# Early fp16 tanh from partial sums and earlier injections in the last 73 Runge-Kutta steps of a conv, mixture and ODE block

## The reference, cut to what matters

```
def _mlp(y, W1, b1, W2, b2, W3, b3):
    h = jnp.tanh(y @ W1.T + b1)
    h = jnp.tanh(h @ W2.T + b2)
    return h @ W3.T + b3
def _rk4_step(y, dt, params):
    k1 = f(y)
    k2 = f(y + dt / 2 * k1)
    k3 = f(y + dt / 2 * k2)
    k4 = f(y + dt * k3)
    return y + dt * (k1 + 2 * k2 + 2 * k3 + k4) / 6
t = t + ode(layernorm(t))      # 16 images x 128 channels, hidden 512, 255 steps one after the other
```

## Time and profile before

| | us |
|---|---|
| median of 3 runs | 2869.14 (2864.23 to 2873.52) |
| profiled execution | 2866.97 |
| its span | 2864.70 |
| PE busy | 2798.6 (98%) |
| DVE busy | 2348.9 (82%) |
| ACT busy | 1553.5 (54%) |
| POOL busy | 774.5 (27%) |
| stretch of the plain steps with their entry, from 2121.4 to 2853.4 | 732.0 |

### The profile page before, as it was taken

How to read it: one execution, slowest core, us unless ns; L and a number is a source line. 1 busy time by engine, 2 the same in 40 slices (tenths; PEclk the granted TensorE clock), 3 DMA queues, 4 the chain that set the end, 5 groups by cost and what they waited for, 6 DMA issues and landing times.

```text
span 2864.7 us, 207841 instructions
## 1 busy us (share of the span) xinstructions
PE 2798.6 (98%) x81958; PEld 2399.7 (84%) x81958; DVE 2348.9 (82%) x13248; ACT 1553.5 (54%) x10132; POOL 774.5 (27%) x1393
## 2 busy tenths in 40 slices
PE   8799999999999999999999999999999999999999
PEld 4578888888888888888888887888889999999998
DVE  5688888888888888888888887888878888888887
ACT  7555555555555555555554444444445555555555
POOL 5833233233233233323322000111122222222222
PEclk9789999999999999999999999999999999999999
DMA  3000000000000000000000000000000000000000
GB/s 119 3 14 11 11 15 11 11 15 11 11 14 12 11 11 15 11 11 15 11 11 9 0 0 1 0 0 0 0 17 0 0 0 0 0 0 0 0 0 15
DMA packets 21984, 28.24 MB, mean 10 GB/s; under 512 B 4384, under 2 KB 12896, under 8 KB 21544
## 3 DMA queue, kind: packets, MB, share of 16 engines
q1 hardware_dynamic: 21928, 27.48, 3.1%
HBM read 25.24 MB, written 2.23 MB: 10 GB/s over the span
## 4 chain that ended last, share of the span: by engine, by line
PE 93%; DVE 3%; ACT 2%; issue 1%; DMA 0%; SPq 0%; POOLq 0%; DVEq 0%; POOL 0%; ACTq 0%
PE PSUM L702 23%; PE PSUM L708 21%; PE PSUM L910 17%; PE PSUM L763 12%; PE PSUM L693 5%; PE PSUM L906 4%; DVE PSUM L1427 1%; PE PSUM L800 1%; PE PSUM L866 1%; PE PSUM L871 1%; PE PSUM L729 1%; ACT HA L1100 1%; PE PSUM L733 1%; PE PSUM L770 1%; PE PSUM L523 0%
## 5 line engine op out<-in xcount | busy, mean ns | idle before, releaser
L1427 DVE TENSOR_REDUCE PSUM<-PSUM 128x32 f32<-128x64 f32 x2912 | 624.8, 232 | 97.4 <-PE PSUM L708 51.9
L702 PEld LDWEIGHTS PSUM<-HA,RL 128*128 128x128 f16 x11648 | 396.2, 96 | 205.8 <-ACT HA L1100 194.7
L1101 ACT ACTIVATE PSUM<-PSUM 128x32 f32<-128x32 f32 x2912 | 561.2, 194 | 0.0
L1100 ACT ACTIVATE HA<-PSUM 128x32 f16<-128x32 f32 x1456 | 289.0, 199 | 472.1 <-DVE PSUM L1427 472.0
L1100 ACT ACTIVATE HB<-PSUM 128x32 f16<-128x32 f32 x1456 | 289.2, 200 | 465.6 <-DVE PSUM L1427 465.5
L702 PE MATMUL PSUM<-HA,RL 128*128 128x16 f16 x11648 | 511.9, 170 | 15.5 <-ACT HA L1100 7.6
L702 PE MATMUL PSUM<-HB,RLU 128*128 128x16 f16 x11648 | 511.4, 170 | 3.7
L435 POOL TENSOR_TENSOR G<-G 128x512 f16<-128x512 f32 x256 | 296.9, 1160 | 683.1 <-ACT G L1073 683.1
L708 PE MATMUL PSUM<-HA,RH 128*128 128x32 f16 x11648 | 465.7, 177 | 0.0
L708 PE MATMUL PSUM<-HB,RHU 128*128 128x32 f16 x11648 | 464.4, 177 | 0.0
L702 PEld LDWEIGHTS PSUM<-HB,RLU 128*128 128x128 f16 x11648 | 393.8, 96 | 46.9 <-ACT HB L1100 2.0
(11 more groups left out here) (315 smaller groups left out, 6726.8 us busy)
## 6 DMA issues: line engine op xcount, KB each, us to landing
G<-scores SPq DMA_DIRECT2D x64, 256.0 KB, 3.1
N<-in_x SPq DMA_DIRECT2D x8, 256.0 KB, 4.7
NHL<-in_w SPq DMA_DIRECT2D x1, 2048.0 KB, 9.9
STF<-in_w SPq DMA_DIRECT2D x1, 2048.0 KB, 14.5
out<-W2HL SPq DMA_DIRECT2D x8, 256.0 KB, 2.4
G<-in_r SPq DMA_DIRECT2D x1, 1024.0 KB, 5.1
R1K<-in_r SPq DMA_DIRECT2D x1, 256.0 KB, 2.7
R3F<-in_r SPq DMA_DIRECT2D x1, 256.0 KB, 5.3
```

The costliest lines, as they stand in the source:

```text
L702: mm(out[m // 2][:, 2 * B * (m % 2):2 * B * (m % 2) + B], lo[:, k, m], src[:, k, 0], start=False, stop=False)
L1100: A(hi[:, 2 * h:2 * h + 2, 0], src, ACT.Tanh, scale=1.0 / scale).then_inc(rk_hi, 1)
L1101: A(full, src, ACT.Tanh, scale=1.0 / scale).then_inc(rk_f, 1)
L1427: v.tensor_reduce(bank[:, SUM:SUM + 2 * B].rearrange("p (m b) -> p m b", m=2), bank[:, 0:4 * B].rearrange("p (m c b) -> p m b c", m=2, c=2 ...
```

## The change

PE has a new order of the 40 products, in which the eight `l` stand last (places 32 to 39), and the other products of m = 0 and 1 end at place 19 (`h30`). The semaphore `sp_p[g]` now counts the end of a group without its `l`; a new one, `sp_all`, the end of the `l`. Ahead of the first `l`, PE waits until ACT has made the fp16 tanh of m0 and m1 of the next layer (`sp_hi[0]`, count + 1), since the `l` add to the sums that this tanh reads. The next layer's injection moves from between the layers to place 32, ahead of the `l`, or to place 36, after four of them, where j = 3 and in lay 0 of j = 0: three of the eight layers. The injection for the first layer of the next step is at the end of the loop's body, and one for the first plain step ahead of the loop.

ACT makes the fp16 tanh of m0 and m1 from sums without their `l`, that of m2 from the high half of its pair alone (without the low half, and without DVE's addition), and that of m3 from the full sum, as before. The full tanh follow, in the order m3, m0 and m1, m2. The low half, which is the difference of the two, takes up what the early tanh left out. DVE adds m3's pair first and m2's after ACT's early tanh of m2, subtracts in the order m3, m0 and m1, m2, and in lay 1 of j = 2 makes `FS` ahead of both additions to y instead of between them.

```diff
 SPLIT_ORDER = [(w[0], int(w[1]), int(w[2])) for w in (
-    "L11 L10 h00 L13 L00 h10 h11 h01 L01 L02 L12 h20 L21 L20 l10 l00 H12 l01 L32 h31 L30 h21 l11 l21 L31 H22 l20 "
...
+    "L03 L02 L11 L22 h10 L21 L20 h11 L23 L10 L30 h31 h20 h00 h21 h01 L00 L01 L31 h30 "
+    "L12 H33 L32 L33 L13 H13 H12 H03 H02 H23 H22 H32 l30 l00 l20 l21 l11 l01 l10 l31").split()]
+OPEN_NEXT_AT = (32, 36)
...
-            def split_layer(s, j, lay, hi, lo, src, opening):
-                waited = set()
+            def split_layer(s, j, lay, hi, lo, src, opening, open_next):
+                waited, after_read = set(), False
                 for i, (kind, k, m) in enumerate(SPLIT_ORDER):
+                    if i == OPEN_NEXT_AT[j == 3 or (j == 0 and lay == 0)]:
+                        open_next()
...
+                    if kind == "l" and not after_read:
+                        after_read = True
+                        pe.wait_ge(sp_hi[0], split_count(s, j, lay) + 1)
+                    rest = [(a, b) for a, _, b in SPLIT_ORDER[i + 1:] if SPLIT_OF[b] == SPLIT_OF[m]]
+                    ends = all((a == "l") != (kind == "l") for a, _ in rest)
...
-                        t.then_inc(sp_p[SPLIT_OF[m]], 1)
+                        t.then_inc(sp_all if kind == "l" else sp_p[SPLIT_OF[m]], 1)
+
+            def open_second(s, j):
+                pe.wait_ge(rk_s, 4 * s + j)
+                split_inject(1, IDV, CI[:, 3], True)
+
+            def open_first(s, j):
+                if j == 1:
+                    pe.wait_ge(rk_hs, s)
+                    state_high()
+                if j == 2:
+                    state_low()
+                pe.wait_ge(rk_u, 4 * s + j + 1)
+                if j in (0, 3):
+                    open_high(UZ if j == 0 else BZ, UI if j == 0 else BI)
+                else:
+                    if j == 2:
+                        pe.wait_ge(x_bl, s - S_PLAIN + 1)
+                    split_inject(0, IDU, UI if j == 1 else IB, True)
 
             def split_step(s, opening):
                 for j in range(4):
-                    pe.wait_ge(rk_s, 4 * s + j)
-                    split_inject(1, IDV, CI[:, 3], True)
-                    split_layer(s, j, 0, RH2, RL2, HA, opening and j == 0)
...
-                    split_layer(s, j, 1, RHU[:, COEF_OF[j]], RLU[:, COEF_OF[j]], HB, False)
-
+                    split_layer(s, j, 0, RH2, RL2, HA, opening and j == 0, lambda: open_first(s, j))
+                    split_layer(s, j, 1, RHU[:, COEF_OF[j]], RLU[:, COEF_OF[j]], HB, False,
+                                lambda: open_second(s, j + 1))
+
+            open_second(S_PLAIN, 0)
             split_step(S_PLAIN, True)
...
-                        for g, ms in enumerate(SPLIT):
-                            act.wait_ge((sp_r if g else sp_p)[g], split_count(s, j, lay))
-                            sl = slice(ms[0], ms[-1] + 1)
-                            A(hi[:, sl, 0], SPLIT_SUM[lay][:, sl], ACT.Tanh, scale=1.0 / scale).then_inc(sp_hi[g], 1)
+                        act.wait_ge(sp_p[0], split_count(s, j, lay))
+                        A(hi[:, 0:2, 0], SPLIT_SUM[lay][:, 0:2], ACT.Tanh, scale=1.0 / scale).then_inc(sp_hi[0], 1)
+                        act.wait_ge(sp_p[1], split_count(s, j, lay))
+                        A(hi[:, 2, 0], PAIRED[lay][0][:, 0:B], ACT.Tanh, scale=1.0 / scale).then_inc(sp_hi[1], 1)
+                        act.wait_ge(sp_r[2], split_count(s, j, lay))
+                        A(hi[:, 3, 0], SPLIT_SUM[lay][:, 3], ACT.Tanh, scale=1.0 / scale).then_inc(sp_hi[2], 1)
+                        for g, done in ((2, sp_r[2]), (0, sp_all), (1, sp_r[1])):
+                            act.wait_ge(done, split_count(s, j, lay))
+                            sl = slice(SPLIT[g][0], SPLIT[g][-1] + 1)
                             A(SPLIT_FULL[lay][:, sl], SPLIT_SUM[lay][:, sl], ACT.Tanh, scale=1.0 / scale).then_inc(sp_f[g], 1)
...
-                            for g in (1, 2):
+                            for g, ready in ((2, sp_p[2]), (1, sp_hi[1])):
                                 ms = SPLIT[g]
-                                dve.wait_ge(sp_p[g], split_count(s, j, lay))
+                                dve.wait_ge(ready, split_count(s, j, lay))
...
-                            for g, ms in enumerate(SPLIT):
+                            for g in (2, 0, 1):
...
-                            if j == 2:
-                                state(s)
...
                             if j == 2:
+                                state(s)
                                 state_end(s)
```

More of the change, by code:

```diff
@@ L90 @@
 SPLIT_ORDER = [(w[0], int(w[1]), int(w[2])) for w in (
-    "L11 L10 h00 L13 L00 h10 h11 h01 L01 L02 L12 h20 L21 L20 l10 l00 H12 l01 L32 h31 L30 h21 l11 l21 L31 H22 l20 "
-    "h30 H02 l30 l31 H32 L22 L03 H23 H33 H03 H13 L23 L33").split()]
+    "L03 L02 L11 L22 h10 L21 L20 h11 L23 L10 L30 h31 h20 h00 h21 h01 L00 L01 L31 h30 "
+    "L12 H33 L32 L33 L13 H13 H12 H03 H02 H23 H22 H32 l30 l00 l20 l21 l11 l01 l10 l31").split()]
+OPEN_NEXT_AT = (32, 36)
 def build(nc, scores, x, wkq, wv, wr, bkq, bv, br, wg, w1, b1, w2, b2, ck, cb, r1, r2, r3, r3n, rb1, rb2, rb3, ident,
@@ L260, in build @@
         sp_p, sp_r, sp_hi, sp_f, sp_lo = ([sem(f"sp_{k}{g}") for g in range(3)] for k in ("p", "r", "hi", "f", "lo"))
+        sp_all = sem("sp_all")
         def split_count(s, j, lay):
@@ L902, in split_layer @@
                             pe.wait_ge((sp_lo if low_half else sp_hi)[group], split_count(s, j, lay))
-                    ends = all(SPLIT_OF[m] != SPLIT_OF[b] for _, _, b in SPLIT_ORDER[i + 1:])
+                    if kind == "l" and not after_read:
[3 more added lines that the diff above has]
+                    ends = all((a == "l") != (kind == "l") for a, _ in rest)
                     if kind == "H":
@@ L909, in split_layer @@
                         half = src[:, k, 1 if kind == "l" else 0].unsqueeze(1).to_broadcast([128, copies, B])
-                        t = mm(repeated(1 - lay, m, B, copies), (lo if kind == "L" else hi)[:, k, m], half, start=False, stop=ends)
+                        t = mm(repeated(1 - lay, m, B, copies), (lo if kind == "L" else hi)[:, k, m], half, start=False,
+                               stop=ends, skip_group_check=kind == "l")
                     if ends:
-                        t.then_inc(sp_p[SPLIT_OF[m]], 1)
+                        t.then_inc(sp_all if kind == "l" else sp_p[SPLIT_OF[m]], 1)
@@ L914, in split_step @@
             def split_step(s, opening):
                 for j in range(4):
-                    pe.wait_ge(rk_s, 4 * s + j)
-                    split_inject(1, IDV, CI[:, 3], True)
-                    split_layer(s, j, 0, RH2, RL2, HA, opening and j == 0)
-                    if j == 1:
-                        pe.wait_ge(rk_hs, s)
-                        state_high()
-                    if j == 2:
-                        state_low()
-                    pe.wait_ge(rk_u, 4 * s + j + 1)
-                    if j in (0, 3):
-                        open_high(UZ if j == 0 else BZ, UI if j == 0 else BI)
-                    else:
-                        if j == 2:
-                            pe.wait_ge(x_bl, s - S_PLAIN + 1)
-                        split_inject(0, IDU, UI if j == 1 else IB, True)
@@ L1147, in _ @@
                 split_step(s, False)
+            act.wait_ge(sp_p[0], split_count(STEPS, 0, 0))
+            A(HA[:, 0:2, 0], SPLIT_SUM[0][:, 0:2], ACT.Tanh, scale=1.0 / SCALE_U).then_inc(sp_hi[0], 1)
             for i in range(OG):
```

## The result

| | before | after |
|---|---|---|
| median of 6 runs | 2869.15 us (2861.86 to 2873.52) | 2886.23 us (2880.84 to 2890.59) |
| ratio to before, 95% interval | 1 | 1.006 (1.0047 to 1.0073) |
| profiled execution, its span | 2866.97, 2864.7 | 2882.18, 2879.9 |
| one plain step | 10.03 us | 10.26 us |

The account below looks back on a forecast made before the run. PE's waits, 0.80 us a step over 9.23 of plain issue, were taken as the bound; 0.46 + 0.19 + 0.09 + 0.16 + 0.20 = 1.10 (used as 1.08), 0.28 longer, 20.4 us in 73 steps: 2888 us, range 2872 to 2900.

Parts of the forecast that it names:

- What bounds the kernel: PE in the plain steps: step length counts, not clock or memory; waits of 0.80 us in 10.03 us a step.
- The floor: PE's plain issue in a step without waits: 364 matmuls at 0.0254, 9.23 us.
- The gate: PE ahead of the first `l`: waits for the early tanh of m0 and m1, 0.46 us a step.
- The hand-over of 0.46: From the product completing m0 and m1 through ACT's tanh to PE's product reading it: 0.21 plus 0.25 us.
- The low half: PE at place 25, lay 1 of j = 1 and 2: low half of m0 and m1 late, 0.045 us each.
- `rk_s`: Injection at place 32 waits for DVE's `FS`: late by 0.045 us, 0.09 for j = 1 and 2.
- DVE's bare wait: DVE between its additions to y, behind lay 1 of j = 2: delays m3 in j = 3, 0.14 us.
- The loop's end: End of PE's loop body, 8 products and 4 injections behind the last binding wait: 0.20 us a step.
- an end that costs nothing: Rival: PE's sequencer takes the branch while products wait in their queue; 0.20 us a step less, 2873 us, chance 0.05.
- The counts in series: Rival: each count PE computes between binding waits costs 0.02 us in eight layers, 0.16 more, 2899 us, chance 0.17.

Follow-up runs that it names:

- experiments 1 and 2: Changed kernel with every injection back behind its layer: 2909.46 us; changed kernel with the sixteen products of m0 and m1 without `l` first: 2863.89 us.
- experiment 3: Changed kernel with DVE's first addition to y ahead of `FS` again: 2887.95 us; changed kernel with both additions moved into j = 3: 2880.56 us.
- experiment 5: PE's loop body with three steps: changed kernel 3053.88 us, kernel before 3047.63 us; with two steps: 2877.80 us and 2865.47 us.

## Why the prediction was right

The forecast was 2888 us in a range of 2872 to 2900; 2886.23 was measured. The mechanism is what was measured: each term has its gap in the table, and the runs show the four that they touch. That the time came within 2 us is in part luck, since two terms were a little too small and four too large. The terms as the prediction shows them add to 1.10, and nothing that it shows gives the 1.08 that it goes on with; 1.10 makes 2889 from the profiled execution, inside the range as well.

- **What bounds the kernel.** Reading starts instead of busy time found 0.80 of waits in a step that the page calls 98% busy. The floor held: 10.26 less 1.03 is 9.23.
- **The gate.** The hand-over of 0.46, read where ACT had been idle, is 0.46 again in three kernels, and the price follows the number of products in between (experiments 1 and 2): 0.475 against 0.46.
- **The low half and `rk_s`.** 0.064 and 0.076 against 0.09 and 0.09. The link that was too long is full tanh to subtraction: I took 0.24 for 32 columns, and in the kernel after it is 0.21 in these layers, as for 16, while the subtraction of 32 columns lasts 0.19 instead of 0.18. That makes 0.67 for 0.685 from the last `l` to place 25, and 0.88 for 0.91 to the injection. In the earlier trace rows DVE had not been idle: the second of the two additions at 2162.14 (0.38 for the pair, 0.20 for one) starts at 2162.32, and the subtraction 0.10 behind it, which is DVE's own spacing.
- **DVE's bare wait.** 0.109 against 0.14 in j = 3. The chain was right, link by link (0.13, 0.26 for 0.28, 0.10 for 0.09), and experiment 3 shows it on the path from both sides. It came out 0.03 shorter over all.
- **The loop's end.** 0.214 against 0.20, and 0.22 by taking it away (experiment 5). Its rival, an end that costs nothing, is out.
- **The counts in series,** the rival at 2899, don't show: 0.16 a step was its price, and the terms of the table leave nothing over the floor.

What the forecast missed together is 0.05 a step (10.31 against 10.26), 4 us, on the side of too long.
